# Queries and keys stacked on two 64-row halves of TensorE's array, in all attention stages of a six-stage transformer kernel

## The chip, the cores and the metric

The kernel runs on one core of one Trainium2 chip. The metric is the device time of one execution in microseconds (us), lower is better. Its engines work side by side and meet at semaphores: TensorE (PE in the profile, its weight loads PEld), VectorE (DVE), ScalarE (ACT), GpSimd (POOL), and SyncE (SP), which here only issues DMAs.

## The reference: what is computed

The input x is 16 x 256 x 128 (batch B, positions T, channels C), in fp32. Six stages follow each other, named here as in the profile:

- f and f (stages 1 and 3): a routed feed-forward, 8 experts, top 2, with capacity.
- r (stage 2): retention. 16 heads of 8 channels; `scores = q @ k.T * decay mask`, no softmax, then `scores @ v`, a group norm and a gate.
- f4a and f6a (in stages 4 and 6): attention with relative positions, 16 heads of 8 channels. `ac = q @ k.T`; `bd[i, j] = q_i . p(i - j)`, with p a projection of sines and cosines; `softmax((ac + bd) * scale) @ v`. Each is followed by a mixture of 32 experts, top 4 (f4m, f6m).
- a (stage 5): plain softmax attention, 16 heads of 8 channels.

Queries and keys are needed close to fp32 accuracy. A query number is split into three bf16 parts, a key likewise, and six products of parts stand for one fp32 product: `QSLOT = (0, 0, 0, 1, 1, 2)`, `KSLOT = (0, 1, 2, 0, 1, 0)`. So each head's contraction is over 6 slots x 8 channels = 48 rows (`USED`), all bf16.

## The kernel before, in words

A batch of 256 positions is worked through in 16 rounds n = 0..15; work of several batches overlaps, each engine having its order written out by hand, one round after the other. Nothing reorders it: an engine runs its list and waits on semaphores. PSUM tiles are rings of 2 or 3 banks.

**Stacks.** Per batch, SP writes the bf16 parts to a scratch in HBM (`write_slots`, L953 to L958, six DMAs) and reads them back as stacks (L1055, L1712, L2194: two DMAs, one into `qs`, one into `ks`), partition = slot x channel, with heads and positions along the row. Rows 0 to 47 hold data, rows 48 to 95 hold zeros, and products are over `0:ROWS` = 96 rows. The zeros are written by memsets in stage f (L779, L863 to L873) or copied by a DMA in stage a.

**Relative attention (`relative_attention`, L2550).** In each round PE does: small pieces of projections (`small`); `relate` for a round five ahead (L2664: two products, 96 rows, 256 columns, positions' weights `w.ws` times queries, into bank `ur`); `scores` (two heads: one bf16 product of queries and keys, L2676, and three products in fp32r of the rotated positions, L2679 to L2681, added in bank `sr`); `turn_round` of the round two back (L2691, four transposes); and in each fourth round `values` (L2704, 16 products of 32 columns of the array each). DVE does in each round `rotate` (L2878, reads `ur`), `maxima` (L2870, reads `sr`) and small pieces; ACT the exponentials (L2804) and copies; POOL adds and rests of `rr` (L3007, L3013).

**Plain attention (`plain_attention`, L1609).** PE does in each round: `scores` (L1739, two products, 96 rows), of which only the row maxima are used (DVE L2006, two banks of `sr`); `project` (eight small pieces per batch); `turned`, 18 rounds later (L1756: the same products with queries and keys exchanged, over `KROWS` = 120 rows, the last 24 of which subtract the maxima, as ones and picks in the keys and three-part maxima in the queries); in each fourth round `values` (L1772). The maxima are split on POOL (L2079 to L2088), transposed by PE (L1785), copied by ACT and moved into the stack by SP (L1695).

**Retention (`retention`, L985).** In each even round PE does four products of four heads (L1070, 96 rows, 128 columns, bank `sd`), every other time four more (L1080, `so`); then a piece of the projections, if one is due (L1108 to L1159); in each fourth round `values` (L1093, L1097, 32 columns of the array each).

Of the kernel before, what the change touches and what calls it, by code (L numbers as in the profile page):

```python
# [28 lines left out]
P = 128  # L29
# [16 lines left out]
ROWS = 96  # L46
KROWS = ROWS + 3 * H // 2
# [67 lines left out]
def routed_ffn(nc, tag, x_sb, k, w):  # L115
# [9 lines left out]
    with ExitStack() as ctx:  # L125
# [20 lines left out]
        stack = [k.qs[:, n, :, :].rearrange("p h t -> p (h t)").bitcast(F32) for n in range(2)]  # L146
# [41 lines left out]
        def ring(name):  # L188
# [7 lines left out]
         mask_step, off_ready, d_ready, g_ready, padded, xt_ready, h1_ready, zeroed, ks_zeroed) = [a.sem(n) for n in (  # L196
             "ln_stats ln_aggr ln_veps ln_rstd xn_ready top_ready lg_ready ex_ready den_step sc_ready best_step "
             "mask_step off_ready d_ready g_ready padded xt_ready h1_ready zeroed ks_zeroed").split()]
# [393 lines left out]
        def _(dve):  # L592
# [145 lines left out]
            for s in range(G + 3):  # L738
# [36 lines left out]
                else:  # L775
                    if closed:
                        residual(q - 1, 0)
                    if s == G + 2:
                        nc.vector.memset(stack[0][32:64, :], 0.0)  # L779
# [33 lines left out]
        def _(pool):  # L813
# [34 lines left out]
            for s in range(G + 1):  # L848
# [11 lines left out]
                if s == 1 and w.load is not None:  # L860
                    pool.wait_ge(h1_ready, 3 * KH)
                    for n, rows in enumerate((slice(32, 64), slice(64, ROWS))):
                        nc.gpsimd.memset(w.ws[rows, :, :, :].rearrange("p a h t -> p (a h t)"), 0.0).then_inc(w.ws_zeroed, 1)  # L863
                        pool.wait_ge(w.ws_zeroed, n + 1)
            pool.wait_ge(g_ready, G)
            if w.load is not None:
                for n, rows in enumerate((slice(32, 64), slice(64, ROWS))):
                    nc.gpsimd.memset(k.ks[rows, :, :, :].rearrange("p a h t -> p (a h t)"), 0.0).then_inc(ks_zeroed, 1)
                    pool.wait_ge(ks_zeroed, n + 1)
            for n, (last, tile, rows) in enumerate((((G // 2 - 2, 1), stack[1], slice(32, 64)), ((G // 2 - 2, 1), stack[1], slice(64, ROWS)),  # L870
                                                    ((G // 2 - 1, 0), stack[0], slice(64, ROWS)))):
                EXPERT[1].full(pool, "back", last)
                nc.gpsimd.memset(tile[rows, :], 0.0).then_inc(zeroed, 1)  # L873
                pool.wait_ge(zeroed, n + 1)
# [63 lines left out]
STACKED = 16 * 2 * len(RUNS)  # L938


def slots_of(part, run, each, n):

    return bass.AP(part.tensor, part.offset, [[each, run], [H * n, HD], [1, H * n]])


USED = 6 * HD
BOUNCED, LANDED = 16 * 6, 16 * 2


# [659 lines left out]
def plain_attention(nc, tag, x_sb, k, io, begun, lead, room):  # L1609
# [8 lines left out]
    with ExitStack() as ctx:  # L1618
# [108 lines left out]
        def _(pe):  # L1727
            def scores(i, n):
# [4 lines left out]
                if g == 2 * NS:  # L1733
                    pe.wait_ge(third_clear, 32)
# [1898 lines left out]
```

## Time and profile before

| | |
|---|---|
| median of 3 runs | 2753.72 us |
| lowest, highest | 2753.01, 2758.3 us |
| profiled execution: span from first to last instruction | 2756.7 us |
| instructions | 60632 |
| mean granted TensorE clock | 0.967 |

The page of the profile gives one execution. Busy times are counted per engine. A matmul's duration includes its way through the array, so two that follow each other overlap in the record: what one costs PE is the distance from its start to the next one's start. The shapes read stationary x moving: "96*128 96x256" is a weight of 96 rows and 128 columns, with 256 columns streamed. Where the stages lie: f until about 297 us, r until 505, f until 800, f4a from 825 to 1397, f4m until 1640, a from 1647 to 1930, f6a from 1937 to 2511, f6m to the end.

### The profile page before, as it was taken

The page shows a single profiled execution, that of the slowest core. Times are in us where ns is not written, and L with a number is a line of the kernel's source. Part 1 is how long each engine was busy: PE and PEld are TensorE (multiplying, and loading weights), DVE is VectorE, ACT ScalarE, POOL GpSimd, SP SyncE. Part 2 cuts the span into 40 slices and gives each one's busy share as a digit, 9 for nine tenths or more (in the row PEclk, how much of TensorE's full clock was granted, in tenths as well). Part 3 has the DMA queues.
Part 4 walks back from the last instruction along what each step waited for, and adds up shares of the span by engine and source line. Part 5 has one row for each costly group of instructions (what it writes and reads, how often), then busy time and mean ns, then how long its engine had stood idle before and what let it go on. Part 6 is the DMA issues. An engine that isn't in the chain of part 4 may idle for free. (4 is left out here: it accounts for less than half of the span.)

```text
span 2756.7 us, 60632 instructions
## 1 busy us (share of the span) xinstructions
PE 2491.5 (90%) x19804; PEld 1926.5 (70%) x19804; DVE 1958.6 (71%) x4716; ACT 1626.3 (59%) x4737; POOL 1666.1 (60%) x2470
## 2 busy tenths in 40 slices
PE   7999699799969999999977988998899999997898
PEld 5788567578858877777777445665787777776743
DVE  5554488455548999999954566775789999996545
ACT  3333244233329888888842335777798888885222
POOL 4322666333226688888842764553668888884366
PEclk9999899899979999999989998999999999998999
DMA  3810366460012222222335236553222222242622
GB/s 120 322 66 1 83 142 139 148 257 1 1 33 47 49 62 62 61 63 60 102 95 160 52 76 137 108 116 69 47 47 61 62 61 53 50 122 65 181 62 68
DMA packets 231992, 242.00 MB, mean 88 GB/s; under 512 B 27538, under 2 KB 203922, under 8 KB 224498
## 3 DMA queue, kind: packets, MB, share of 16 engines
q1 hardware_dynamic: 182530, 196.14, 27.6%
q0 software_dynamic: 12288, 25.19, 3.4%
q10 hardware_dynamic: 36864, 16.79, 2.1%
q8 instruction: 163, 2.67, 0.4%
q14 instruction: 147, 1.20, 0.2%
HBM read 99.28 MB, written 134.41 MB: 85 GB/s over the span
## 5 line engine op out<-in xcount | busy, mean ns | idle before, releaser
L2804 ACT ACTIVATE f4a_pr<-f4a_sr,f4a_nm 128x256 f32<-128x256 f32 x512 | 238.9, 479 | 52.1 <-DVE f4a_nm L2870 51.8
L2804 ACT ACTIVATE f6a_pr<-f6a_sr,f6a_nm 128x256 f32<-128x256 f32 x512 | 238.8, 479 | 50.1 <-DVE f6a_nm L2870 49.7
L3007 POOL TENSOR_TENSOR f4a_rr<-a5b_room 128x256 f32<-128x256 f32 x256 | 195.7, 765 | 81.1 <-DVE a5b_room L2878 74.0
L3007 POOL TENSOR_TENSOR f6a_rr<-a5b_room 128x256 f32<-128x256 f32 x256 | 195.4, 763 | 74.2 <-DVE a5b_room L2878 67.5
L2006 DVE TENSOR_REDUCE a_nm<-a_sr 128x2 f32<-128x512 f32 x256 | 166.8, 684 | 69.8 <-PE a_sr L1739 68.8
L2878 DVE TENSOR_TENSOR a5b_room<-f4a_ur,f4a_turn 128x512 f32<-128x512 f32 x256 | 174.0, 680 | 32.7 <-PE f4a_ur L2664 30.9
L2878 DVE TENSOR_TENSOR a5b_room<-f6a_ur,f6l_turn 128x512 f32<-128x512 f32 x256 | 174.0, 680 | 27.1 <-PE f6a_ur L2664 25.4
L2679 PE MATMUL f6a_sr<-f6l_pe_hi,f6a_rr_hi 128*128 128x256 f32 x512 | 187.7, 367 | 0.0
L2679 PE MATMUL f4a_sr<-f4a_pe_hi,f4a_rr_hi 128*128 128x256 f32 x512 | 187.7, 367 | 0.0
L2870 DVE TENSOR_REDUCE f4a_nm<-f4a_sr 128x2 f32<-128x512 f32 x256 | 174.6, 682 | 18.1 <-PE f4a_sr L2681 17.8
L2870 DVE TENSOR_REDUCE f6a_nm<-f6a_sr 128x2 f32<-128x512 f32 x256 | 174.5, 682 | 17.3 <-PE f6a_sr L2681 16.9
L2676 PE MATMUL f6a_sr<-all_ks,all_qs 96*128 96x256 bf16 x512 | 143.5, 280 | 16.2 <-ACT f6a_pr L2804 13.7
L2676 PE MATMUL f4a_sr<-all_ks,all_qs 96*128 96x256 bf16 x512 | 143.5, 280 | 14.8 <-ACT f4a_pr L2804 12.7
L2691 PE MATMUL f6a_tr<-all_table,f6a_pr 128*128 128x128 f32 x1024 | 153.3, 272 | 0.0
L2691 PE MATMUL f4a_tr<-all_table,f4a_pr 128*128 128x128 f32 x1024 | 153.3, 272 | 0.0
L3013 POOL TENSOR_TENSOR f6a_rr_lo<-f6a_rr,f6a_rr_hi 128x256 fp32r<-128x256 f32 x192 | 147.1, 767 | 0.0
L3013 POOL TENSOR_TENSOR f4a_rr_lo<-f4a_rr,f4a_rr_hi 128x256 fp32r<-128x256 f32 x192 | 146.8, 765 | 0.0
L2681 PE MATMUL f6a_sr<-f6l_pe_hi,f6a_rr_lo 128*128 128x256 f32 x512 | 144.9, 283 | 0.0
L2681 PE MATMUL f4a_sr<-f4a_pe_hi,f4a_rr_lo 128*128 128x256 f32 x512 | 144.8, 283 | 0.0
L2680 PE MATMUL f4a_sr<-f4a_pe_lo,f4a_rr_hi 128*128 128x256 f32 x512 | 144.8, 283 | 0.0
L2680 PE MATMUL f6a_sr<-f6l_pe_lo,f6a_rr_hi 128*128 128x256 f32 x512 | 144.7, 283 | 0.0
L2789 ACT ACTIVATE f6a_pts<-f6a_tr 128x512 f32<-128x512 f32 x208 | 124.8, 600 | 16.4 <-PE f6a_tr L2691 15.5
(634 smaller groups left out, 8261.1 us busy)
## 6 DMA issues: line engine op xcount, KB each, us to landing
slots<-f_zero SPq DMA_DIRECT2D x100, 512.0 KB
f4m_xr<-slots SPq DMA_DIRECT2D x128, 64.0 KB, 2.2
slots<-f4m_y ACTq DMA_DIRECT2D x128, 64.0 KB, 2.2
f6m_xr<-slots SPq DMA_DIRECT2D x128, 64.0 KB, 2.2
slots<-f6m_y ACTq DMA_DIRECT2D x128, 64.0 KB, 2.3
r_scratch<-r_parts SPq DMA_DIRECT2D x32, 192.0 KB, 2.3
all_qs<-r_scratch SPq DMA_DIRECT2D x16, 384.0 KB, 4.9
all_ks<-r_scratch SPq DMA_DIRECT2D x16, 384.0 KB, 6.8
```

The source lines that it names most:

```text
L2006: nc.vector.tensor_reduce(nm[:, r // 2, t, at_:at_ + 2], sr[:, g % SB, :].rearrange("p (x s) -> p x s", x=2), AX.X, ALU.max, negate=True). ...
L2676: nc.tensor.matmul(out, qs[0:ROWS, lead.buffer(b[0]), h, t * P:(t + 1) * P], ks[0:ROWS, lead.buffer(b[0]), h, :], start=True, stop=False)
L2679: nc.tensor.matmul(out, rr_hi[at], pe_hi[:, :], start=False, stop=False)
L2680: nc.tensor.matmul(out, rr_hi[at], pe_lo[:, :], start=False, stop=False)
L2681: mm = nc.tensor.matmul(out, rr_lo[at], pe_hi[:, :], start=False, stop=True)
L2691: mm = nc.tensor.transpose(ring.bank(b, n // 2)[:, o:o + P], pr[:, n % 4, x, st * P:(st + 1) * P], k.ident)
L2789: return nc.scalar.activation(dst, src_, ACT.Copy)
L2804: last = nc.scalar.activation(pr[:, n % 4, x, :], sr.bank(b, n)[:, x * T:(x + 1) * T], ACT.Exp, bias=nm[:, n % SB, x:x + 1], accum_out=zs[ ...
L2870: nc.vector.tensor_reduce(nm[:, n % SB, :], sr.bank(b, n).rearrange("p (x s) -> p x s", x=2), AX.X, ALU.max, negate=True).then_inc(nm_read ...
L2878: nc.vector.tensor_tensor(tmp[:, hs % 2, :, :], ur.bank(b, hs).rearrange("p (u t) -> p u t", u=2), turn[:, :, :], ALU.mult).then_inc(ur.em ...
L3007: nc.gpsimd.tensor_tensor(rr[:, hs % RAW, :], tmp[:, hs % 2, 0, :], tmp[:, hs % 2, 1, :], ALU.add)\
L3013: nc.gpsimd.tensor_tensor(rr_lo[:, hs % RRS, :], rr[:, hs % RAW, :], rr_hi[:, hs % RRS, :], ALU.subtract)\
```

## The change

The 16 heads are laid in two halves: one half's 48 rows stand at partitions 0 to 47, the other's at 64 to 111, with 8 heads along each row. The contraction of a product is then over 48 rows (60 in `turned`: 48 and 12) that begin at partition 0 or 64, instead of 96 (120) from partition 0.

- Names: `ROWS` and `KROWS` go; `HS` = 8, `TILE` = 64, `USED` = 48, `TOP` = 12; `rows(g)` is the slice of a half.
- The zero rows go: the memsets L779 and L863 to L873 and the DMA copies of zeros.
- Each read of a stack is four DMAs instead of two, one for each half of queries and of keys; the bytes are the same. The weights `w.ws` are loaded by 12 DMAs instead of 6; the ones of stage a by 6 instead of 2, and moves of maxima there by two DMAs of 12 rows and 4 heads instead of one of 24 rows and 8 heads.
- Order on PE in f4a and f6a: the two products of `relate` and the two bf16 products of `scores` go in turns (content, relate, content, relate), always on opposite halves, into different banks; then the six fp32r products. Both waits (for `ur` and for `sr`) stand ahead of the first of the four. `AHEAD` is 6 instead of 5.
- Order on PE in stage a: the products of `scores` and `turned` go in turns on opposite halves, ahead of `project`; both waits stand ahead of them. Heads, columns of the maxima and their split are numbered to match.
- Retention: the same products in the same order, each round r on half r % 2, four or eight after each other on the same half. Inputs' columns are permuted on the host to match.

```diff
-ROWS = 96
-KROWS = ROWS + 3 * H // 2
+HS = H // 2
+TILE = 64
+USED = SLOTS * HD
+TOP = 3 * QUAD
...
+def rows(g, first=0, number=USED):
+    return slice(g * TILE + first, g * TILE + first + number)
+
+def read_slots(sp, tiles, scratch, stacked):
+    for u, dst in enumerate(tiles):
+        slots = scratch[u].rearrange("n (d g h) t -> g (n d) (h t)", g=2, h=HS)
+        for g in range(2):
+            sp.dma_start(dst[rows(g), :, :].rearrange("s h t -> s (h t)"), slots[g]).then_inc(stacked, 16)
...
 (retention, scores)
+                own = rows(r % 2)
                 for j in range(QUAD):
-                    h = j * QUAD + r
-                    mm = nc.tensor.matmul(sd[:, n % DB, j, :], ks[0:ROWS, par, h, block_], qs[0:ROWS, par, h, block_], start=True,
-                                          stop=True)
+                    h = r // 2 * QUAD + j
+                    mm = nc.tensor.matmul(sd[:, n % DB, j, :], ks[own, par, h, block_], qs[own, par, h, block_], start=True, stop=True)
...
 (plain_attention, the tensor engine's round)
                 for n in range(NS):
-                    i = batch(s, 2)
+                    i, (e, m) = batch(s, 2), late(s, n)
                     if i is not None:
-                        scores(i, n)
+                        scores_room(i, n)
+                    if e is not None:
+                        turned_room(e, m)
+                    for x in range(2):
+                        if i is not None:
+                            scores(i, n, x)
+                        if e is not None:
+                            turned(e, m, x)
                     project(s, n)
-                    for m in range(NS):
-                        i = at(s, n, TURNED + m)
-                        if i is not None:
-                            turned(i, m)
...
 (relative_attention)
-    NR, RRS, AHEAD, RAW = 16, 8, 5, 4
+    NR, RRS, AHEAD, RAW = 16, 8, 6, 4
...
+            def products(it, n):
+                (b, hs), i = relating(it, n), attend(it)
                 if b is not None:
-                    relate(b, hs)
+                    relate_room(b, hs)
+                if i:
+                    pe.wait_ge(sr.emptied, sr.nth(i, n))
+                for x in range(2):
+                    if i:
+                        contents(i, n, x)
+                    if b is not None:
+                        relate(b, hs, x)
+                if i:
+                    positions(i, n)
...
-                        nc.vector.memset(stack[0][32:64, :], 0.0)
```

## Rows read from the trace of the kernel before

**Rows 1.** Windows: steady stretches of r, f4a, a; stretch, us, PE, PEld, DVE, ACT, POOL.
```profile
340.00:490.00 150.00, 139.56 (x1846) 105.79 (x1846) 125.38 (x301) 74.39 (x187) 97.44 (x136) 1.00 0.68 142
950.00:1350.00 400.00, 375.14 (x3460) 311.42 (x3459) 378.26 (x850) 351.58 (x1181) 344.97 (x485) 1.00 0.26 61
1700.00:1900.00 200.00, 188.33 (x1874) 125.52 (x1874) 148.25 (x320) 145.91 (x324) 106.45 (x250) 0.99 0.53 106
```

**Rows 2.** Waits in 950 to 1350 us: who for whom, us, times, longest.
```profile
PE f4a_desk L2253 <- DVE f4o_s L2946: 10.4, 10, 1.2
PE f4a_sr L2676 <- ACT f4a_pr L2804: 8.5, 22, 0.7
...
DVE f4a_nm L2870 <- PE f4a_sr L2681: 7.8, 31, 0.3
```

**Rows 3.** Timeline, PE, one round of f4a: start us, duration, line, shapes.
```profile
1204.40 0.60 PE L2691 MATMUL f4a_tr<-all_table,f4a_pr 128*128 128x128 f32 x4
1204.84 0.38 PE L2664 MATMUL f4a_ur<-all_qs,all_ws 96*128 96x256 bf16 x2
1205.06 0.27 PE L2676 MATMUL f4a_sr<-all_ks,all_qs 96*128 96x256 bf16 x1
...
1205.54 0.28 PE L2676 MATMUL f4a_sr<-all_ks,all_qs 96*128 96x256 bf16 x1
...
1206.03 0.60 PE L2691 MATMUL f4a_tr<-all_table,f4a_pr 128*128 128x128 f32 x4
```

**Rows 4.** Timeline, PE, f4a: into the 32-column products and out of them.
```profile
1191.05 0.60 PE L2691 MATMUL f4a_tr<-all_table,f4a_pr 128*128 128x128 f32 x4
1191.58 1.07 PE L2704 MATMUL f4a_y<-f4a_pts,f4a_vm 128*32 128x256 f32 x16
1192.58 0.71 PE L2266 MATMUL f4a_desk<-f4a_wq,f4a_xt 128*128 128x128 f32 x4
1193.12 0.38 PE L2664 MATMUL f4a_ur<-all_qs,all_ws 96*128 96x256 bf16 x2
```

**Rows 5.** Timeline, PE, f4a: a product of 32 rows and 64 columns.
```profile
1381.97 0.20 PE L2522 MATMUL f4a_desk<-f4o_ends,f4o_spread 32*128 32x64 bf16 x1
1382.10 0.39 PE L2664 MATMUL f4a_ur<-all_qs,all_ws 96*128 96x256 bf16 x2
```

**Rows 6.** Timeline, PE, stage a: rounds without 32-column products.
```profile
1785.36 0.38 PE L1756 MATMUL a_st<-all_qs,all_ks 120*128 120x256 bf16 x2
1785.58 0.38 PE L1739 MATMUL a_sr<-a_k,a_q 96*128 96x256 bf16 x2
1785.80 0.61 PE L1801 MATMUL a_desk<-a5b_room,a_xt 128*128 128x128 f32 x4
1786.25 0.28 PE L1756 MATMUL a_st<-all_qs,all_ks 120*128 120x256 bf16 x1
```

**Rows 7.** Timeline, DVE, stage a: two maxima after each other.
```profile
1790.18 1.29 DVE L2006 TENSOR_REDUCE a_nm<-a_sr 128x2 f32<-128x512 f32 x2 [1.20 <-PE a_sr L1739]
```

**Rows 8.** Timeline, PE, retention: products and pieces of the projections.
```profile
448.97 1.13 PE L1127 MATMUL r_desk<-r_xt,r_w 128*128 128x256 f32 x4
449.94 0.39 PE L1070 MATMUL r_sd<-all_qs,all_ks 96*128 96x128 bf16 x4
450.17 0.39 PE L1080 MATMUL r_so<-all_qs,all_ks 96*128 96x128 bf16 x4
450.39 1.08 PE L1140 MATMUL r_desk<-r_xt,r_w 128*128 128x256 f32 x4
451.31 0.39 PE L1070 MATMUL r_sd<-all_qs,all_ks 96*128 96x128 bf16 x4
```

**Rows 9.** Waits of PE in 340 to 490 us, retention.
```profile
PE r_desk L1154 <- DVE r_qv L1321: 9.5, 13, 0.8
PE r_sd L1070 <- DMA all_ks<-r_scratch: 0.7, 1, 0.7
```

**Rows 10.** Timeline, DVE: a memset of zeros at the end of stage 1.
```profile
293.49 1.76 DVE L779 MEMSET all_qs<- 32x2048 f32 x1 [0.48 <-issue]
```

More of the change, by code:

```diff
@@ L859, in _ @@
                         rest_of_h1(s + 1, m)
[L860 to L864, printed above, removed]
-            pool.wait_ge(g_ready, G)
[L866 to L874, printed above, removed]
+            pool.wait_ge(g_ready, G)
 class Desk:
@@ L1683, in _ @@
             begun.read(sp, 1)
-            for tile, zeros in ((q3, k.qs), (k3, k.ks)):
-                sp.dma_start(tile[USED:ROWS, :, :], zeros[USED:ROWS, 0, :, :]).then_inc(third_clear, 16)
             sp.wait_ge(ones_set, 2)
-            for tile in (k.ks[ROWS:KROWS, 1, :, :], k3[ROWS:KROWS, :, :]):
-                sp.dma_start(tile, k.ks[ROWS:KROWS, 0, :, :]).then_inc(ones_copied, 16)
+            for i in range(NB):
+                for g in range(2):
+                    sp.dma_start(keys(i)[rows(g, USED, TOP), :, :], ones).then_inc(ones_copied, 16)
             def move(i, half):
@@ L2077, in split_maxima @@
                 whole = nm[:, half, :, :]
-                first, second, third = (mf[:, half, :, n * HALF:(n + 1) * HALF] for n in range(3))
+                first, second, third = (mf[:, half, :, 0:2 * TOP].rearrange("p t (g n j) -> p n t g j", g=2, n=3)[:, n] for n in range(3))
+                by_tile = "p t (g j) -> p t g j"
+                whole4, r4, b4 = [v.rearrange(by_tile, g=2) for v in (whole, r1[:, :, :], b2[:, :, :])]
                 nc.gpsimd.tensor_copy(b1[:, :, :], whole).then_inc(split, 1)
@@ L2660, in relate, with contents, positions @@
                 pe.wait_ge(ur.emptied, ur.nth(b, hs))
-                out = ur.bank(b, hs)
+            def relate(b, hs, u):
                 h = head_at(hs)
-                for u in range(2):
-                    mm = nc.tensor.matmul(out[:, u * T:(u + 1) * T], w.ws[:, u, h, :], qs[0:ROWS, lead.buffer(b[0]), h, :],
-                                          start=True, stop=True)
-                mm.then_inc(ur.filled, 1)
-            def scores(b, n):
-                r, jj, t = n // QUAD, n // 2 % 2, n % 2
-                pe.wait_ge(sr.emptied, sr.nth(b, n))
+                own = rows(h // HS)
+                mm = nc.tensor.matmul(ur.bank(b, hs)[:, u * T:(u + 1) * T], w.ws[own, u, h % HS, :],
+                                      qs[own, lead.buffer(b[0]), h % HS, :], start=True, stop=True)
+                if u:
+                    mm.then_inc(ur.filled, 1)
+            def contents(b, n, x):
+                r, jj, t = n // QUAD, n // 2 % 2, n % 2
+                own, h = rows(jj), x * QUAD + r
+                nc.tensor.matmul(sr.bank(b, n)[:, x * T:(x + 1) * T], qs[own, lead.buffer(b[0]), h, t * P:(t + 1) * P],
+                                 ks[own, lead.buffer(b[0]), h, :], start=(x == 0), stop=False, skip_group_check=True)
+            def positions(b, n):
+                t = n % 2
                 if t == 0:
@@ L2755, in step @@
                     small(it, n)
[L2756 to L2758 removed]
+                    products(it, n)
                     b, m = turning(it, n)
@@ L2769, in _ @@
             pe.wait_ge(k.loaded, k.loaded_count)
-            run(step, related)
+            run(step, products)
         def take_turned(eng, b, n, copy):
```

151 lines of the change are left out of this document (69 added, 82 removed).

## Prediction

> **What bounds the kernel now.** I looked first where the stages lie and how full each engine is in their steady parts. In relative attention (570 us of f4a and as much of f6a; 950 to 1350 stands for both) PE is busy 375.1 of 400 us and DVE 378.3, ACT 351.6 [rows 1]: two engines near their limit, coupled by rings of two banks. In retention PE is busy 139.6 of 150 us, the next (DVE) 125.4. In stage a PE has 188.3 of 200, DVE 148.3. So PE's list decides in r and a, PE and DVE together in f4a and f6a. The table of waits is next: in 400 us PE waits 10.4 us for DVE and 8.5 for ACT, DVE 7.8 for PE's scores [rows 2]. A busy PE is not yet a PE at its peak, so the third view is the timeline, read from start to start, for the price of each product.
>
> **Prices on PE.** One round of f4a [rows 3]: four transposes 0.44 us (1204.40 to 1204.84), two `relate` 0.22, a bf16 product with three fp32r ones 0.48 (1205.06 to 1205.54), the same again 0.49. A bf16 product of 256 columns is thus 0.11 and an fp32r one (0.48 - 0.11) / 3 = 0.12. The part that the change touches, from 1204.84 to 1206.03, takes 1.19 us.
>
> Changing the array's division has a price already. The four transposes before `values` should take 0.44, but the 32-column products begin 0.53 after them [rows 4]: 0.09 to go in. Going out: the four products of L2266 take 0.54 (1192.58 to 1193.12) where the same kind, L1801, takes 0.45 with no division changed before it [rows 6]: 0.09 to 0.10 more, because the first fp32 weights of 128 columns are loaded with nothing in front of them. And the way out itself: the 16 products stream as four groups of 0.216 (a 256-column fp32 product, 0.97 less 0.10 over four in L1127, [rows 8]), 0.86, but the next start is 1.00 after the first, so 0.14, of which I give 0.04 to the starts inside a group: 0.10. Is that so for a division by rows too? The one product in the trace that uses few rows (32 rows, 64 columns) is followed after 0.13 us [rows 5]; at 0.055 for 128 columns (four in 0.23, [rows 8]) its columns need 0.03. Again 0.10 is left. I take 0.09 in, 0.10 out, and 0.10 for the first fp32 or fp32r load after it (0.05 for transposes, half of it). Bounds: 0 for each, since no row shows a 64-row division; above, 0.13 in or out, the whole step of rows 5.
>
> The Trainium skill, "TensorEngine Tiling (Array Packing)", Key Properties, says that changing the tiling mode, not just the tile, drains the engine. It names every mode, so it speaks for carrying the 0.09 and 0.10 over to halves of 64 rows, and so against this change, which changes mode twice in each round; it moves my chance, no term of the sum.
>
> **Do two halves run side by side?** No row shows it for rows of the array; for columns it does: 16 products of 256 columns in about four streams' time, so four at once [rows 4]. I take a pair as one stream plus a little, 0.115 us, the low end being 0.11 and the high end 0.22, no overlap.
>
> **f4a and f6a.** Per round after the change: in 0.09, two pairs 0.23, out 0.10, first fp32r load 0.10, six fp32r products 6 x 0.12 = 0.72: 1.24 against 1.19. What 0.22 us of overlap gives, three switching costs of together 0.29 take back. Times 16 rounds PE gets 0.8 us longer per batch (the four `values` are entered from the transposes and left into a small piece as before, no change). PE waits for others at 18.9 us of 400 [rows 2], and a longer list fills such waits first; also DVE, equally full, starves sooner, because `relate` now stands behind the wait for `sr` and `rotate` gets its bank later. I take three quarters: 0.6 us per batch, 16 batches, two stages: +19 us. Ends: 0 (all absorbed) and 1.1 with that delay, +35.
>
> **Stage a.** Two and two products take 0.22 + 0.22 us per round [rows 6]; two pairs 0.23 save 0.22, 3.5 us per batch. Added per batch: `project` has eight pieces, each now left into from a 64-row part: 8 x 0.10 out, 5 first loads of transposes at 0.05 and 3 of fp32 weights at 0.10, and six ways back in at 0.09 (two pieces are followed by `values`, whose entry is paid today): 1.9 us. PE gets 1.6 us shorter. But six rounds of 16 have neither piece nor values; they take 0.44 on PE today and cannot go faster than DVE's maximum, 0.60 from one to the next (two in 1.29, one lasts 0.69, [rows 7]): their 6 x 0.22 = 1.3 is lost, `split` and its transposes wait for the same maxima. Left: 0.3 us x 15 batches = -5 us. Ends -24 (rival A) and +8 (a whole 0.5 us per batch of the added switching comes through, the gain being lost at the rings).
>
> **Retention.** Nothing overlaps here: four or eight products in a row are on one half. PE gets only switches. Today four `values` per batch, in and out: 8. After: L1108, L1127, L1140, L1147, L1116, L1159 and the two small ones (L1133, L1154) all break the 64-row parts; counted round by round 18 changes, 10 more at 0.09 to 0.10 = 0.94. The first load is partly bare already (L1140 takes 0.92 for 4 x 0.216 = 0.86, [rows 8]); 0.05 more in three places, 0.15. PE waits 9.5 us in 13 batches for `qv` [rows 9], a chain that starts on PE and takes up one switch, 0.09. Sum +1.0 us per batch; PE has no other slack, so 15 x 1.0 = +15 us. Ends 0 and +20.
>
> **Cheap edits.** Reads of stacks: the same bytes in twice the DMAs; PE waits 0.7 us in 150 for them [rows 9], the fetch being one batch ahead; SP's queue gets two more issues per batch ahead of the next write, nothing, or up to 1 us per batch if that cover were gone in r. The moves of maxima shrink to half the bytes, one issue later; PE reaches them seven rounds on. Without the zeros, DVE's 1.76 us memset just before its last addition [rows 10] goes, but that addition then waits for PE's last products, which run into the same microsecond: 0.3 us in each of two stages, -0.5. The ones of stage a are needed 18 rounds in. POOL's memsets stand in front of an idle POOL: nothing.
>
> **Sum.** 19 - 5 + 15 - 0.5 = +28.5 us on the profiled span of 2756.7, 2785.2; the page gives no other time for that execution, and its span lies 3.0 above the median of the runs, so 2782.
>
> **Rivals.**
> A, a division into halves of rows costs nothing to change. For it: all 128 columns stay in use and no row shows a 64-row one; against it: rows 5. A round of f4a is then 0.23 + 0.72 = 0.95, PE 3.9 us per batch shorter, and DVE takes over as the bound. It has 400 - 378.3 = 21.7 us idle in 400, 2 per batch; I take 1.1 back, 32 batches, -35. Stage a: 3.5 less 1.3, with the rings 1.6, -24. Retention 0. Time 2694: faster, where I forecast slower. It decides from 0.24 us of switching per round downwards.
> B, the pairs don't overlap (the change doesn't do what it says). Then each round has 0.22 more: f4a 0.27 x 16 = 4.3 per batch, 85% through, 3.7 x 32 = 119; stage a +1.9 x 15 = 28; retention 15. 2915. Against it: the column products do overlap.
> C, switching costs only 0.09 and 0.10, the first loads are hidden. A round takes 1.14, 0.8 less per batch, -19 in all; stage a -13; retention +14: 2736.
> D, in a 64-row division the next weights don't load under a product on the same half. Four products of one bank now go at 0.055 each [rows 8], their loads therefore hidden behind products on the same rows. With a load bare, bounded by 0.05 to 0.10 per product as with the first loads above, retention's 48 products per batch get 2.4 to 4.8 us longer: +36 to +72 more, 2854 at the top. The Trainium skill, "TensorE: Matmul & The Clock Gate", Part 3, The mechanism, states such a rule for LDWEIGHTS: it overlaps with matmuls in flight only where the row group differs. The trace disagrees for the undivided array.
>
> **How the numbers follow.** Forecast (with its own range 2755 to 2810) 0.48, A 0.25, C 0.13, B 0.10, D 0.04. The range of 8 in 10 reaches down to most of A and up past the upper ends above: 2690 to 2822; B, D and a part of A stay out. A measurement tells 0.2% (5.5 us) from nothing. Faster: A 0.25, C 0.07, forecast 0.02: 0.34. Same 0.08 (C 0.03, forecast 0.05). Slower 0.58.
>
> **What would show it.** In the timeline of the changed kernel: the last transpose to the first content product 0.20 instead of 0.11 (A: 0.11); content and relate starting within 0.02 of each other (B: 0.11); the last pair to the first fp32r product 0.20, and 0.2 more than 0.12 to the second (C: 0.12). The retention's batches (13 of them in 150 us) longer by 1.0 us each; stage a a few us shorter in all; f4a about 10 longer, with DVE's busy time the same and its waits for `ur` (L2664) up. The forecast is wrong if the first fp32r product follows the pair without a gap, or if stage a gains over 15 us.

## The result, and the profile after

The changed kernel takes 2825.82 us (median of 4 runs, 2817.85 to 2837.58); the kernel before took 2753.36 in the runs beside them. The ratio is 1.0257, with a 95% interval of 1.0238 to 1.0276: slower by 72 us, where +29 was forecast and 2822 was the upper end of the range. The profiled execution is the shortest of the four (2817.85; span 2816.0), 59.3 us over the profiled span of before. Three lines of its profile's page: the span, PE's busy time, and the granted clock in 40 slices.

```profile
span 2816.0 us, 61442 instructions
PE 2532.8 (90%) x19804; PEld 1783.7 (63%) x19804; DVE 1956.8 (69%) x4714; ACT 1626.5 (58%) x4737; POOL 1617.6 (57%) x2460
PEclk9999898799989999999999998999899999998999
```

First the 59.3 us by stage, each from the first or last product of a stage (its `sd`, `sr` or 32-column products) in the timelines of both:

| stretch | before | after | difference | forecast |
|---|---|---|---|---|
| start to r's first product | 326.8 | 320.3 | -6.5 | -0.3 |
| r, to its last values | 177.3 | 204.4 | +27.1 | +15 |
| f, to f4a's first scores | 321.2 | 321.2 | 0 | -0.2 |
| f4a, to its last values | 576.1 | 593.7 | +17.6 | half of 19 |
| f4m | 245.4 | 242.3 | -3.1 | 0 |
| a | 277.9 | 284.9 | +7.0 | -5 |
| a to f6a | 12.9 | 13.2 | +0.3 | 0 |
| f6a | 576.6 | 596.8 | +20.2 | half of 19 |
| f6m, to the end | 242.5 | 239.2 | -3.3 | 0 |

Then windows of the three kinds of stages: stretch, its length, busy time of PE, PEld, DVE, ACT, POOL, the granted clock, DMA share, GB/s. These answer to [rows 1].

```profile
326.00:388.00 62.00, 59.22 (x718) 39.92 (x721) 48.59 (x116) 28.89 (x73) 38.49 (x54) 1.00 0.54 135
388.00:496.00 108.00, 103.59 (x1082) 66.85 (x1074) 74.46 (x177) 43.06 (x110) 58.34 (x84) 0.87 0.47 118
950.00:1350.00 400.00, 368.89 (x3357) 269.63 (x3357) 370.09 (x828) 342.14 (x1149) 328.76 (x474) 1.00 0.21 58
1712.00:1760.00 48.00, 41.92 (x466) 20.60 (x468) 36.96 (x81) 35.73 (x80) 25.88 (x61) 1.00 0.43 109
1760.00:1940.00 180.00, 156.83 (x1574) 74.15 (x1571) 124.51 (x269) 123.48 (x274) 89.90 (x211) 0.90 0.39 94
```

The reader is to see two things. In r and a the clock is 1.00 at first, and later 0.87 and 0.90; before it was 1.00 and 0.99 there. And in f4a, at full clock, neither PE (368.9 of 400 us; 375.1 before) nor DVE (370.1; 378.3) is as busy as it was, though each batch takes longer: both wait more. A batch, from its first 32-column product to the next one's, takes in steady state

| | before | after |
|---|---|---|
| r | 11.24 | 12.07, from the sixth on 13.67 |
| f4a, f6a | 36.55 | 37.83 |
| a | 15.98 | 15.83, from the fourth on 17.18 |

The timeline of PE in f4a, one round (start, duration, line, shapes), against [rows 3]:

```profile
1201.09 0.60 PE L2693 MATMUL f4a_tr<-all_table,f4a_pr 128*128 128x128 f32 x4
1201.62 0.28 PE L2671 MATMUL f4a_sr<-all_ks,all_qs 48*128 48x256 bf16 x1
1201.62 0.28 PE L2663 MATMUL f4a_ur<-all_qs,all_ws 48*128 48x256 bf16 x1
1201.74 0.27 PE L2671 MATMUL f4a_sr<-all_ks,all_qs 48*128 48x256 bf16 x1
1201.74 0.27 PE L2663 MATMUL f4a_ur<-all_qs,all_ws 48*128 48x256 bf16 x1
1201.94 0.38 PE L2681 MATMUL f4a_sr<-f4a_pe_hi,f4a_rr_hi 128*128 128x256 f32 x1
1202.17 0.28 PE L2682 MATMUL f4a_sr<-f4a_pe_lo,f4a_rr_hi 128*128 128x256 f32 x1
...
1202.75 0.60 PE L2693 MATMUL f4a_tr<-all_table,f4a_pr 128*128 128x128 f32 x4
```

Content and relate start together (medians over 340 pairs: 4 ns apart). From the transposes' start to the pair 0.53 us instead of 0.44: 0.09 to go in. From the second pair to the first fp32r product 0.20, so 0.08 to go out; that product to the next 0.23 instead of 0.12: 0.11 for the first load. In all 1.13 us from the first pair to the next transposes, and 0.09 before it. A round of nothing but these products, in which PE waits for nobody, takes 1.66 us; before it took 1.62. The waits of f4a from 950 to 1350 us (who for whom, total, times, longest), against [rows 2]. L3016 is GpSimd's sum of the rotated positions, L2671 PE's scores, L2887 DVE's rotation (`rotate`), which reads what `relate` wrote:

```profile
POOL f4a_rr L3016 <- DVE a5b_room L2887: 49.8, 47, 2.1
PE f4a_sr L2671 <- ACT f4a_pr L2813: 22.5, 39, 1.1
DVE a5b_room L2887 <- PE f4a_ur L2663: 18.3, 32, 1.0
```

PE's wait for the scores' bank went from 8.5 to 22.5 us, and DVE's for relate from 7.7 to 18.3. Last, retention on PE, and the clock there. Product after product on the same half comes after 0.055 us (four in 0.22, 376.26 to 376.49), as in [rows 8]. L1122 takes 1.13 us in one batch and 2.08 in the next. Around the second one (389.5 to 393) the clock is 0.52, and in the next fall (404 to 406) 0.50, that is at 1.2 GHz of its two levels:

```profile
376.26 0.40 PE L1066 MATMUL r_sd<-all_qs,all_ks 48*128 48x128 bf16 x4
376.49 0.38 PE L1075 MATMUL r_so<-all_qs,all_ks 48*128 48x128 bf16 x4
376.81 0.44 PE L1103 MATMUL r_desk<-all_table,r_xn 128*128 128x128 f32 x2
...
378.29 1.13 PE L1122 MATMUL r_desk<-r_xt,r_w 128*128 128x256 f32 x4
...
391.01 2.08 PE L1122 MATMUL r_desk<-r_xt,r_w 128*128 128x256 f32 x4
```
```profile
389.50:393.00 3.50, 3.50 (x23) 1.78 (x20) 1.52 (x8) 1.29 (x3) 2.56 (x5) 0.52 0.82 224
393.00:403.00 10.00, 9.38 (x115) 6.52 (x115) 7.84 (x15) 4.08 (x11) 4.95 (x7) 1.00 0.34 81
404.00:406.00 2.00, 2.00 (x15) 1.34 (x8) 0.77 (x2) 0.57 (x1) 1.82 (x4) 0.50 0.95 254
407.00:416.00 9.00, 8.38 (x106) 5.81 (x104) 7.28 (x14) 4.08 (x11) 4.35 (x5) 1.00 0.36 95
```

So in this execution the clock is at its lower level for some 3.4 us of every 13.67 from the sixth batch on, and at full rate for the rest. When it starts to fall isn't fixed: relate_first, halves_ahead5 and halves_apart (below) have the same retention code, and their steady batches take the same 12.07 or 13.67 us, but there the clock fell seven, four and four times instead of eight. The low stretch at the start of their retention was longer (20 to 27 us against 7), and retention as a whole took 204 to 211 us.

### The profile page after: what moved, and what is told of

It reads as the page before. It is cut to its first block and busy times, and to the rows that moved or that the text cites. A ratio compares the mean times of both kernels' runs of the same rounds, so it can differ in the third digit from the quotient of the medians.

```text
span 2816.0 us, 61442 instructions
## 1 busy us (share of the span) xinstructions
PE 2532.8 (90%) x19804; PEld 1783.7 (63%) x19804; DVE 1956.8 (69%) x4714; ACT 1626.5 (58%) x4737; POOL 1617.6 (57%) x2460
## 5 line engine op out<-in xcount | busy, mean ns | idle before, releaser
L3016 POOL TENSOR_TENSOR f4a_rr<-a5b_room 128x256 f32<-128x256 f32 x256 | 191.5, 750 | 104.6 <-DVE a5b_room L2887 101.0
L3016 POOL TENSOR_TENSOR f6a_rr<-a5b_room 128x256 f32<-128x256 f32 x256 | 190.7, 748 | 101.0 <-DVE a5b_room L2887 97.5
L2887 DVE TENSOR_TENSOR a5b_room<-f4a_ur,f4a_turn 128x512 f32<-128x512 f32 x256 | 173.9, 680 | 47.9 <-PE f4a_ur L2663 46.0
L2887 DVE TENSOR_TENSOR a5b_room<-f6a_ur,f6l_turn 128x512 f32<-128x512 f32 x256 | 173.9, 680 | 44.8 <-PE f6a_ur L2663 43.0
L2681 PE MATMUL f6a_sr<-f6l_pe_hi,f6a_rr_hi 128*128 128x256 f32 x512 | 171.9, 336 | 0.0
L2681 PE MATMUL f4a_sr<-f4a_pe_hi,f4a_rr_hi 128*128 128x256 f32 x512 | 171.3, 334 | 0.0
L2798 ACT ACTIVATE f6a_pts<-f6a_tr 128x512 f32<-128x512 f32 x208 | 124.6, 599 | 27.2 <-PE f6a_tr L2693 26.8
L2798 ACT ACTIVATE f4a_pts<-f4a_tr 128x512 f32<-128x512 f32 x208 | 124.6, 599 | 24.7 <-PE f4a_tr L2693 24.2
L2681 PEld LDWEIGHTS f6a_sr<-f6l_pe_hi,f6a_rr_hi 128*128 128x128 f32 x512 | 96.8, 189 | 54.7 <-issue 53.9
```

The source lines that it names most:

```text
L2681: nc.tensor.matmul(out, rr_hi[at], pe_hi[:, :], start=False, stop=False, skip_group_check=True)
L2798: return nc.scalar.activation(dst, src_, ACT.Copy)
L2887: nc.vector.tensor_tensor(tmp[:, hs % 2, :, :], ur.bank(b, hs).rearrange("p (u t) -> p u t", u=2), turn[:, :, :], ALU.mult).then_inc(ur.em ...
L3016: nc.gpsimd.tensor_tensor(rr[:, hs % RAW, :], tmp[:, hs % 2, 0, :], tmp[:, hs % 2, 1, :], ALU.add)\
```

## The experiments

Runs of one group were made on one chip with the kernel before beside them; another group may have another chip (before took 2758 us on some, 2788 on others), so ratios are within a group, and batches, which agree between chips to 0.03 us, are compared across.

**First group** (before 2790.81). all_full: the new order, the array never divided.

```diff
-                own = rows(r % 2)
+                own = slice(0, P)
...
-                own, h = rows(jj), x * QUAD + r
+                own, h = slice(0, P), x * QUAD + r
```

> The changed kernel with its order, its waits and its DMAs, but every product of stacks runs over all 128 rows, so that the array is never divided into halves (rows between the halves are zeroed by memsets). Left out by it: the two heads of a product are added, not kept apart. Theory, the division itself costs, once by changing it and once by the clock that follows: retention's batches go from 12.07 and later 13.67 us to 11.2 throughout with a granted clock of 1.00; f4a's batches from 37.83 to 36.5 to 36.9; stage a's from 17.18 to about 16.0 at 1.00; in all about 60 us less than the changed kernel, some 2755. Rival, the new order and the waits put together ahead of the products cost: f4a's batches stay at 37.5 or more and stage a's above 16.5, some 2790. Rival, the four half reads of each stack cost in retention: its batches stay above 12.

It took 2813.83 us, 1.0089 times before (1.0074 to 1.0103). Batches: r 11.24, a 15.89, f4a 37.75. Windows of r, of a and of f4a:

```profile
330.00:492.00 162.00, 150.15 (x1987) 113.64 (x1980) 134.13 (x321) 77.96 (x195) 102.12 (x145) 0.99 0.55 138
1700.00:1930.00 230.00, 215.99 (x2144) 143.68 (x2143) 173.40 (x370) 170.00 (x373) 121.01 (x286) 0.99 0.42 103
950.00:1350.00 400.00, 362.49 (x3350) 307.11 (x3348) 374.61 (x818) 343.18 (x1149) 333.11 (x473) 1.00 0.22 59
```

For r and a the theory stands: undivided, the time and the clock come back. For f4a and f6a it falls, and with it the prediction's account: a loss of 1.2 us per batch is there without any division. All of it is waiting: PE is busy 34.2 us of a batch (362.5 of 400, times 37.75), as before (34.3), and idle 3.5 instead of 2.3. In the changed kernel PE is busy 34.9 and idle 2.9. (Stage a starts some 14 us late here, since its first scores wait for the added zeros and the ones; that is no part of the change.)

repeats: more work at the same places.

```diff
-                for j in range(QUAD):
+                for j in [*range(QUAD), *range(QUAD)]:
```

> The changed kernel with more work for PE at the same places: in retention each product of queries and keys is issued twice (48 more per batch at 0.055 us), in stage a each product of the turned scores twice (32 more at 0.11 or less); results are written over by the same values. Theory, the granted clock falls in r and a because PE there does less between its changes of division: with the repeats it stays at 1.00, retention's batches come to 12.07 + 2.64 = 14.7 us throughout, stage a's to 15.83 + at most 1.8 = 17.6 or less. Rival, it falls because of the changes of division themselves, of which there are as many: the clock stays at about 0.86 from the middle of r on, retention's batches come to 16 us or more and stage a's to 19.

Batches of r came to 14.06 us, of a to 16.75, and the clock to 1.00 (windows of r and a):

```profile
410.00:540.00 130.00, 130.00 (x1760) 97.26 (x1760) 88.66 (x209) 49.41 (x126) 61.73 (x90) 1.00 0.43 111
1800.00:1960.00 160.00, 151.91 (x1761) 85.68 (x1759) 115.61 (x248) 115.08 (x251) 80.52 (x193) 1.00 0.43 105
```

With as many changes of division and more products, the clock stays up: it fell for want of work, not for the changes as such. Whether it is the gaps around the changes or products on half of the rows that count as less work, no run tells apart. Stage a's batches are 0.43 us shorter than the changed kernel's 17.18 although 32 products more are in them; stage a as a whole is 5.4 us longer, since its start and its last batches lose more than the steady ones gain. Retention's batches are longer than with the lower clock (14.06 against 13.67). (The whole took 2884.36 us, 1.0367 times before.)

relate_first: the waits of f4a apart, the first relate ahead.

```diff
+                        relate(b, hs, x)
+                    if i:
+                        if x == 0:
+                            pe.wait_ge(sr.emptied, sr.nth(i, n))
+                        contents(i, n, x)
```

> The changed kernel, but in f4a and f6a the first product of relate goes ahead of the wait for the scores' bank, and each wait stands right ahead of the first product that needs it. Theory, of the 1.27 us that a batch of f4a got longer 0.9 are PE's own (changes of division) and the rest comes by the coupling of PE and DVE, not by where the waits stand: batches stay at 37.8 within 0.1, the time within 5 us of the changed kernel. Rival, the two waits together hold relate and so DVE's rotation back: batches come to 37.4 or less, the time 12 us or more below it.

Batches 37.84 us; 2851.87 in all, 1.0221 times before (1.0200 to 1.0242), an interval that just meets the changed kernel's. The place of the waits alone isn't it; relate's second product is as late as ever, 0.12 us after the first product of content.

before_light: two side edits of the change without its products.

```diff
-                for u, dst in enumerate((qs, ks)):
-                    sp.dma_start(dst[0:USED, par, :, :]...
+                read_slots(sp, (qs[:, par, :, :], ks[:, par, :, :]), scratch[par], stacked)
...
 (the start, GpSimd)
+                nc.gpsimd.memset(w.ws[rows, :, :, :]...
```

> The kernel before with two things of the change and none of its products: the zeros of the positions' weights are set at the very start and not between two rounds of stage 1, and each stack is read by four DMAs of 24 rows instead of two of 48. Theory: stage 1 ends 3.6 us sooner, as in the changed kernel; first products of retention and of stage a come 2.6 us sooner each because shorter DMAs land sooner; in all 8 to 9 us less than before, 2745. Rival, these came by chance or by the smaller zeros at the stages' ends: no difference over 3 us.

2790.25 us, ratio 0.9995 (0.9984 to 1.0007). A miss, and the trace says why: the 7.07 us of memsets at the start held the stage's first products back by 4.3 us (8.58 to 12.87), and what was gained in the 67th us only paid for that: stage 1's last product came at 292.03 us, against 292.06. Four reads of 24 rows gave 1.0 us, not 2.6.

**Second group** (before 2785.96): which part of the new order costs.

```diff
-    NR, RRS, AHEAD, RAW = 16, 8, 5, 4
+    NR, RRS, AHEAD, RAW = 16, 8, 6, 4
```

> The kernel before with one constant changed: relate runs six rounds ahead instead of five, as in the changed kernel. With the array undivided, the new order made batches of f4a 37.75 us long instead of 36.55, so the order and not the division holds f4a back. Theory, it is the waits put together: relate stands behind the wait for the scores' bank, DVE's rotation comes late, and running six rounds ahead does not matter: f4a's batches stay at 36.55 within 0.15, the time within 5 us of before. Rival, running six rounds ahead shifts DVE's and ACT's lists against PE's and costs the 1.2 us: batches of 37.5 or more, the time 30 us or more over before.

Batches 37.04, the time 2797.20, ratio 1.0037 (1.0024 to 1.0051): six rounds ahead cost 0.5 us per batch with the old order, between both expectations.

The next has the new order with the old constant:

```diff
+                for x in range(2):
+                    if i:
+                        contents(i, n, x)
+                    if b is not None:
+                        relate(b, hs, x)
+                if i:
+                    positions(i, n)
```

> The kernel before with only the new order of f4a and f6a: both waits first, then content, relate, content, relate over 96 rows, then the six fp32r products; relate still five rounds ahead. Theory, the waits put together cost: f4a's batches go to 37.75 or beyond, the time to 38 us or more over before. Rival, the six rounds ahead cost: batches stay at 36.55 to 36.7, the time within 5 us of before.

Batches 37.93, 2823.34 us, ratio 1.0142 (1.0115 to 1.0169): the new order of products alone costs 1.4 us per batch.

And the changed kernel with `AHEAD` 5:

> The changed kernel with relate five rounds ahead instead of six. Theory, the waits put together cost in either case: f4a's batches at 37.8 or above, the time not below the changed kernel's. Rival, the six rounds ahead cost: then PE's own 0.9 us per batch and no more is left, batches of about 37.4 and 12 us less than the changed kernel.

Batches 38.72, 2882.55 us, ratio 1.0359 (1.0328 to 1.0389). Undivided, six rounds ahead help the new order by 0.2 us (37.75 with six in all_full, 37.93 with five). In the halves 0.9 us lie between them, but this run changes more than its expectation says. Content's half and relate's half both alternate every two rounds, so that an even distance and an odd one don't meet the same way: six rounds ahead, the two stand on opposite halves in every round; five ahead, on the same half in every second one, and there nothing overlaps (82 of 165 rounds of f4a):

```profile
1205.43 0.28 PE L2671 MATMUL f4a_sr<-all_ks,all_qs 48*128 48x256 bf16 x1
1205.55 0.27 PE L2663 MATMUL f4a_ur<-all_qs,all_ws 48*128 48x256 bf16 x1
1205.66 0.27 PE L2671 MATMUL f4a_sr<-all_ks,all_qs 48*128 48x256 bf16 x1
1205.77 0.27 PE L2663 MATMUL f4a_ur<-all_qs,all_ws 48*128 48x256 bf16 x1
```

From the first of the four to the first fp32r product it is 0.54 us in such rounds and 0.32 in the others. Eight rounds of 0.21 make PE's list 1.7 us per batch longer (376.9 of 400, times 38.72, are 36.5 us busy, against 34.9). So `AHEAD` 6 isn't a matter of tuning here: the overlap needs it.

> The kernel before once more, for a trace from the same chip as these. All theories expect retention's batches at 11.24, f4a's at 36.55, stage a's at 15.98 us and a granted clock of 1.00 in them; where it is longer than 2756.7 us in all, it is in f4m and f6m, as in the last four kernels, whose f4m and f6m took 15 to 17 us longer each than in the first trace.

One run, 2791.66 us; batches 11.25, 36.57 and 16.00, clock 1.00; f4m and f6m 259 and 261 us instead of 245 and 243. It is the chip that differs, and it does so there.

**Third group** (before 2757.70).

```diff
             def related(it, n):
-                b, hs = relating(it, n)
+                (b, hs), i = relating(it, n), attend(it)
+                if i:
+                    pe.wait_ge(sr.emptied, sr.nth(i, n))
```

> The kernel before, its products and their order unchanged, but PE waits for the scores' bank ahead of relate instead of behind it, in f4a and f6a. Theory, what the new order costs is that relate no longer lies in the time in which PE waits for ScalarE's exponentials, and that DVE gets it later: f4a's batches go from 36.55 to 37.9 as with the whole new order, the time to 36 us or more over before. Rival, going in turns (two open banks, scores finished later) costs: batches stay under 37.0, the time within 12 us of before.

Batches 36.61, 2761.72 us, ratio 1.0024 (1.0013 to 1.0034). The theory fell: relate behind the wait costs nearly nothing (4 us in all) as long as its two products come first after it.

```diff
                 if n:
                     pe.wait_ge(copied, n)
+                    pe.sem_inc(so_filled, 1)
+                    return
```

> The kernel before with less for PE to do in retention and no division into halves: of the products of the off-diagonal block only the first four of all batches are issued, 15 of 16 per batch and more are left out (the scores there are then those of another block), about 0.9 us of PE's 11.24 us per batch, about what changing the division leaves idle in the changed kernel. Theory, the granted clock follows how much PE does: it falls below 1.00 in the second half of r here too, and batches get no shorter than 11.2 us there though 10.4 would do. Rival, it takes the changes of division: the clock stays at 1.00 and batches come to 10.3 to 10.7 us throughout.

Batches 10.97 with one of 12.50; 2753.46 us, ratio 0.9988 (0.9978 to 0.9997). The clock was at 0.86 in two of the stretches of 12 us inside r, where before had none:

```profile
386.00:398.00 12.00, 10.17 (x128) 7.35 (x125) 10.48 (x24) 5.78 (x15) 8.82 (x12) 1.00 0.73 150
398.00:410.00 12.00, 11.31 (x120) 7.89 (x120) 8.94 (x24) 5.38 (x14) 7.16 (x12) 0.86 0.72 145
470.00:482.00 12.00, 10.80 (x134) 7.03 (x134) 9.54 (x20) 5.00 (x13) 5.20 (x7) 0.86 0.67 147
```

Less work brings falls without any division, but two in those stretches, not one per batch; half a confirmation. The batches met neither expectation (11.2 or more, 10.3 to 10.7).

```diff
-                        nc.gpsimd.memset(w.ws[rows, ...].rearrange(...), 0.0).then_inc(w.ws_zeroed, 1)
+                        nc.gpsimd.memset(w.ws[rows, ...].rearrange(...).bitcast(F32), 0.0).then_inc(w.ws_zeroed, 1)
...
+                            scores(i, n, x)
+                        if e is not None:
+                            turned(e, m, x)
```

> The kernel before with what the traces point to: the zeros of the positions' weights and of the keys are written as fp32 words, which halves those memsets (7.06 us for two between rounds of stage 1), and in stage a the products of scores and of turned go in turns ahead of the projections, over whole rows. Theory: stage 1 ends 3.5 us sooner, stage a's batches come to 15.88 instead of 16.0, 1.8 us in all; 5 us less than before. Rival: the start of stage 1 waits for something else within a microsecond of the memset, and stage a's gain goes into a longer start: within 2 us of before.

2753.81 us, ratio 0.9991 (0.9982 to 1.0000), between theory and rival. Stage 1 gave 2.7 us; stage a's batches came to 15.94, but three of them to 16.7 to 16.9, and the new order there gained nothing over the stage.

**Fourth group** (before 2755.54), with the cause in f4a still open.

```diff
+                    for u in range(2):
+                        relate(b, hs, u)
+                if i:
+                    pe.wait_ge(sr.emptied, sr.nth(i, n))
+                    for x in range(2):
+                        contents(i, n, x)
+                    positions(i, n)
```

> The kernel before with only the grouping of the new order in f4a and f6a: relate's two products first, then the wait for the scores' bank, then both bf16 products of content and behind them all six fp32r products. PE needs 0.08 us less per round for it (one way from bf16 to fp32r weights instead of two). Theory now, with the wait cleared: what costs in the new order is that relate's second product ends 0.22 us later and with it DVE's rotation, GpSimd's sum and ScalarE's copy, which stands ahead of the exponentials. Then batches of f4a stay at 36.6 or get shorter here. Rival, the grouping itself costs, since both heads' scores become complete only at the end: batches of 37.5 or more.

```diff
 (scores)
                 for x in range(2):
+                    if x:
+                        between()
 (the round)
-                        scores(attend(it), n)
+                        scores(attend(it), n, lambda: related(it, n))
```

> The kernel before, but relate's two products stand between the first head's four products of scores and the second head's, so that they end 0.5 us later after the wait, later than in the changed kernel's order, with no grouping and no turns. Theory (late relate costs): batches of f4a of 38 us or more. Rival (grouping costs): 36.6 to 36.9.

before_grouped: batches 36.55, 2754.63 us, ratio 0.9994 (0.9984 to 1.0003). before_middle: 38.57, 2810.79 us, ratio 1.0200 (1.0183 to 1.0217). Windows of f4a, of the first and of the second:

```profile
950.00:1350.00 400.00, 371.55 (x3461) 314.44 (x3459) 379.40 (x851) 351.63 (x1181) 345.03 (x485) 1.00 0.26 61
```
```profile
950.00:1350.00 400.00, 358.30 (x3272) 295.32 (x3272) 370.68 (x813) 335.28 (x1121) 321.37 (x466) 1.00 0.24 54
```

and three of the waits of before_middle (GpSimd's sum for the rotation, ScalarE's exponentials for DVE's maxima, the rotation for relate):

```profile
POOL f4a_rr L3010 <- DVE a5b_room L2881: 52.2, 58, 1.9
ACT f4a_pr L2807 <- DVE f4a_nm L2873: 50.6, 51, 1.9
DVE a5b_room L2881 <- PE f4a_ur L2664: 27.2, 42, 1.1
```

This settles it for the undivided array. before_grouped took PE's busy time from 374.9 to 371.6 us, and a round without waits from 1.62 to 1.59 (not by the 0.08 expected), and the batches stayed: PE's own time does not set them. What does is when relate's second product starts after the first product that passed the wait for the scores' bank: ahead of it, batches of 36.55; 0.11 us after it (before_wait_first), 36.61; 0.33 (before_joint), 37.93; 0.60 (before_middle), 38.57. The scores' last product starts equally late in these three, 1.04 to 1.06 us after the wait, so that later scores aren't the cause.

The way from there to PE's wait isn't the one that the expectations name. ScalarE's copy never sat idle for GpSimd's sum in before_joint and before_middle. But in DVE's list each round has the rotation and then, mostly directly behind it, the maxima:

```profile
1204.09 0.69 DVE L2881 TENSOR_TENSOR a5b_room<-f4a_ur,f4a_turn 128x512 f32<-128x512 f32 x1 [0.31 <-PE f4a_ur L2664]
1204.69 0.68 DVE L2873 TENSOR_REDUCE f4a_nm<-f4a_sr 128x2 f32<-128x512 f32 x1
```

The rotation's wait for relate grew with the lateness, from 7.6 us in before_again and before_wait_first to 14.4 in before_joint and 27.2 in before_middle; the exponentials' wait for the maxima went from 37.8 and 33.2 to 44.3 and 50.6. PE's wait for the bank follows the exponentials.

**Fifth group** (before 2788.42).

halves_apart is the changed kernel with `AHEAD` 5 and the `products` of before_grouped.

> The changed kernel, but in f4a and f6a relate goes ahead of the wait for the scores' bank again, five rounds ahead, and so beside nothing: relate, relate, wait, content, content, six fp32r products, all on halves of rows. PE loses what the two overlaps give, 2 x 0.11 us per round or 3.5 per batch, and relate is no longer late. Theory (late relate costs in the halves too, 38.7 us per batch with five rounds ahead and turns): batches of 38.0 or less in spite of the longer list. Rival (in the halves it is PE's own list that decides): 40 us or more.

2857.65 us, ratio 1.0241 (1.0221 to 1.0261). Batches between 37.57 and 38.73, 38.1 on average, against 38.72 with the turns:

```profile
950.00:1350.00 400.00, 388.73 (x3319) 285.69 (x3317) 368.37 (x815) 340.98 (x1138) 327.61 (x468) 1.00 0.21 57
```

PE is busy for 388.7 us instead of 376.9 (halves_ahead5) and the batches are 0.6 us shorter. So late relate costs in the halves too, at least where it is as late as in halves_ahead5 (0.34 us in every second round); now PE's list, at 97% of the stretch, is near its limit. The average missed the 38.0 of the theory by 0.1. One premise of the run is wrong: relate does not stand "beside nothing". In 55 of 168 rounds of f4a, those on opposite halves that had no wait in between, content's products started beside relate's, its first one ahead of relate's second, though both of relate's come first in PE's list:

```profile
1203.26 0.28 PE L2663 MATMUL f4a_ur<-all_qs,all_ws 48*128 48x256 bf16 x1
1203.26 0.28 PE L2671 MATMUL f4a_sr<-all_ks,all_qs 48*128 48x256 bf16 x1
1203.38 0.27 PE L2663 MATMUL f4a_ur<-all_qs,all_ws 48*128 48x256 bf16 x1
1203.38 0.27 PE L2671 MATMUL f4a_sr<-all_ks,all_qs 48*128 48x256 bf16 x1
```

So "nothing reorders it", said of the engines' lists, doesn't hold for the start of products on the two halves, and relate need not stand behind the wait to overlap, where that wait is over by then.

before_words joins before_better's memsets and before_grouped.

> The kernel before with the two harmless edits that the runs found: zeros of the positions' weights and keys written as fp32 words (3.66 us instead of 7.06 between rounds of stage 1) and the fp32r products of both heads grouped behind both contents, relate ahead of the wait. Theory: 2.7 us from stage 1, up to 1 us from the grouping: 3 to 4 us less than before. Rival: within 1 us of before.

2784.65 us, ratio 0.9983 (0.9975 to 0.9992): 3.8 us less than before, faster than both kernels. GpSimd between two rounds of stage 1, in before_again and in before_words:

```profile
66.74 7.07 POOL L863 MEMSET all_ws<- 32x4096 bf16 x2
76.94 0.20 POOL L816 TENSOR_TENSOR f_veps<-f_mv,all_half 128x4 f32<-128x4 f32 x1 [3.14 <-DVE f_mv L605]
```
```profile
66.64 3.66 POOL L863 MEMSET all_ws<- 32x2048 f32 x2
73.44 0.20 POOL L816 TENSOR_TENSOR f_veps<-f_mv,all_half 128x4 f32<-128x4 f32 x1 [3.14 <-DVE f_mv L605]
```

The next work of GpSimd comes 3.5 us sooner, and so do the last product of stage 1 and the first of retention.

## Why the prediction was wrong, point by point

**Right: the prices on PE.** In 0.09, measured 0.09; out 0.10, 0.08; first load 0.10, 0.11; a pair 0.115, 0.12 for the first and then the 0.20 that holds the way out. Retention +1.0 us per batch, +0.83 until the clock fell (0.09 to 0.10 at each change); stage a -0.3, -0.15. A batch of f4a +0.8 on PE, +0.6 (34.3 to 34.9 us busy). The rule on modes of the Trainium skill ("TensorEngine Tiling (Array Packing)", Key Properties: changing the mode drains the array) agrees with these gaps. Rivals A, B and C are out by the same rows, and D by retention's 0.055 us between products on one half; the rule of the Trainium skill behind D ("TensorE: Matmul & The Clock Gate", Part 3, The mechanism: weights load beside matmuls in flight only for another group of rows) isn't borne out here.

**Failed: "retention ... Ends 0 and +20", "Stage a ... Left: 0.3 us".** Both sums took the clock for granted. r gave +27.1: 15 x 0.83 = 12.5 from changes, 8 batches x 1.6 = 12.8 from the clock, the rest at the ends. a gave +7.0: nine batches with 1.35 more from the clock are 12.2, less 1.8 from twelve batches (0.15 each) and 2.7 from its start, which leaves 7.7; its end took the rest. These are the falls of one execution; others had fewer (above). The forecast for the profiled span was 31 us short (+59.3 against +28.5): 25 more from the clock, 19 more from f4a and f6a (below), 6 less at the start and 6 less in f4m and f6m. repeats shows the cause: the same changes of division with more products keep 1.00, and stage a's steady batches even get shorter. PE's busy share in the windows doesn't tell it beforehand: 96% in r before the fall, 92% in f4a, where it never fell. The Trainium skill ("TensorE: Matmul & The Clock Gate", Part 1, What's actually happening) says the gate follows how busy PE has recently been; repeats agrees, the busy shares just given don't.

**Failed: "Times 16 rounds PE gets 0.8 us longer per batch ... I take three quarters".** +37.8 for both stages came where +19 stood, at 1.27 us per batch. Of these 0.6 are PE's own work, about what the prediction let through; the other 0.7 are waits, which it held at nothing in its middle value. all_full has 1.20 of waits with no division at all. The prediction saw the place (`relate` "stands behind the wait for `sr` and `rotate` gets its bank later") and gave it at most 0.3 us, and only for the upper end of its range. before_grouped, before_wait_first, before_joint and before_middle show that undivided it is the whole of the loss, and that it sets in between 0.11 and 0.33 us of lateness. That the changed kernel's 37.83 lies only 0.08 above all_full doesn't show that the division costs 0.08: its relate is less late (0.12 against 0.33) and PE's round longer (1.66 against 1.59), and the two may cancel.

**Failed, small: "POOL's memsets stand in front of an idle POOL: nothing".** GpSimd's idle time by the table of waits came later in that stage; where the memset stood, PE's next round waited for GpSimd. It was worth 3.6 us; in before_words half of the memset's time brought as much as 3.5. 2.6 us more came as retention's first stacks landed sooner; before_light had only 1.0 of it with shorter reads, so the rest is open.

**Median against profile.** The profiled execution was the shortest of its kernel, +59.3; the median gives +72. The longest one had the lowest mean clock (2837.58 at 0.947), but of the others 2822.87 had 0.955 and 2828.78 had 0.952, against 0.954: no clear account, and there is no trace of them.

**What stood in no term.** The forecast's own terms measured about 30 us (12.5 in retention, 19 of PE's own in f4a and f6a, less 2 in stage a), against 28.5 in the sum. What it left out are the 25 us of the clock and the 18 of waits in f4a and f6a. The 12 us that came off at the start and in f4m and f6m weren't foreseen either; it is by them, and so by luck, that the time lies only 4 us above the range.

**Open.** How the changed kernel's 1.27 us per batch divide between late relate and PE's longer list. Its relate's second product starts only 0.12 us after the wait, which undivided and with five rounds ahead cost nearly nothing; yet DVE waits 18.3 us in 400 for relate, more than in before_joint (14.4). Six rounds ahead alone cost 0.5 us in the old order. No run has the changed kernel with relate ahead of the wait and still six rounds ahead, which would tell. Open too are the 3 us by which f4m and f6m each got shorter.

## What to carry to other kernels

Price a change not only by what it adds to an engine's list: in a loop across four engines, ask which result each of them takes next, and how many tenths of a microsecond it may come later; here, undivided, 0.11 cost under 0.1 us per batch and 0.33 cost 1.4, while work taken off PE gave nothing. If an overlap needs two products on opposite halves, count round by round that every distance in the schedule keeps them there. Before you make TensorE's work lighter, or put gaps into it, in a stage where the clock is at 1.00, count what the lower level would cost: in two stages it cost as much as the change itself or more. And write zeros in wide words; on GpSimd a memset of 4096 bf16 per row took 3.5 us and one of 2048 fp32 words, the same bytes, 1.8.

## What the runs showed that I had not expected

- Products on opposite halves of rows start 4 ns apart (340 pairs), into different banks.
- Batches got shorter by idle products: stage a's steady batch with 32 repeated products takes 16.75 us at a clock of 1.00, against 17.18 without them at 0.90 (the stage as a whole gained nothing).
- Products on opposite halves start side by side even where PE's list has both of one half first (55 rounds of halves_apart).
- Six rounds ahead instead of five: +0.5 us per batch with the old order, -0.2 with the new one, both undivided. In the halves it is -0.9, but five rounds ahead lose the overlap in every second round.
